# Seventy bf16 products with constants, whose results nobody reads, put on TensorE at six waits of a transformer kernel

## What is computed

```
x = x + attention(layernorm(x))        # 32 heads of 16, ALiBi bias, causal softmax, projection
x = x + moe(layernorm(x))              # 3 experts (tanh, gelu, silu), 2 of them chosen per batch
x = x + mlp(layernorm(x))              # silu(x Wg) with the half nearest to zero cut per row, times x Wu, times Wd
x = x + moe(layernorm(x))              # the same weights as before

# moe, per batch b: the two experts are those of the first token of the batch
router_input = concatenate([h, text_strength / vision_strength])
scores = softmax(router_input @ gate_w + gate_b)
out = sum_i top_val[i] * (act_e(h @ w1[e] + b1[e]) @ w2[e] + b2[e]),  e = top_idx[first token, i]
```

## Time and profile before

| | |
|---|---|
| time, 3 runs | 722.05, 723.75, 724.3 us; median 723.75 |
| the profiled execution | 721.25 us, of which the span of instructions is 719.5 us |
| TensorE busy | 664.0 us, 92% of the span |
| VectorE, ScalarE, GpSimd busy | 484.1, 338.8, 81.1 us |
| mean granted clock of TensorE | 0.984 of full speed |
| longest waits of TensorE after the first transpose | 3.8 us (L2005), 3.6 (L1627), 3.4 (L1802), 2.3 each (L2024, L1724) |

### The profile page before, as it was taken

The page is one execution under the profiler, slowest core; times in us unless marked ns, Lnnn a source line. Parts: engine busy times, 40 slices in busy tenths (PEclk is TensorE's granted clock), DMA queues, the critical chain, the costliest instruction groups (busy, mean ns, idle before and its releaser), DMA issues.

```text
span 719.5 us, 9856 instructions
## 1 busy us (share of the span) xinstructions
PE 664.0 (92%) x3656; PEld 480.4 (67%) x3656; DVE 484.1 (67%) x905; ACT 338.8 (47%) x520; POOL 81.1 (11%) x185
## 2 busy tenths in 40 slices
PE   4887999999988879999999899999999879999996
PEld 3665677677666557887777565665756555778775
DVE  6647595796589769786794636456365785868555
ACT  4203643612633663532459968466374804435231
POOL 4302002101200020001060010010100300100000
PEclk9989999999999999999999999999999989999999
DMA  8393511521844140000260000000004004000000
GB/s 295 102 267 115 166 46 47 155 67 38 257 148 152 72 158 1 0 1 1 92 221 3 0 1 0 1 2 0 0 1 160 16 0 176 2 29 15 15 30 30
DMA packets 31618, 51.85 MB, mean 72 GB/s; under 512 B 3289, under 2 KB 16988, under 8 KB 30015
## 3 DMA queue, kind: packets, MB, share of 16 engines
q1 hardware_dynamic: 31186, 49.64, 21.5%
q10 hardware_dynamic: 384, 1.57, 1.0%
HBM read 42.61 MB, written 8.40 MB: 71 GB/s over the span
## 4 chain that ended last, share of the span: by engine, by line
PE 77%; DVE 14%; DMA 2%; ACT 2%; issue 2%; SPq 1%; POOL 1%; ACTq 1%; DVEq 0%; POOLq 0%
PE ps L1835 13%; PE ps L1974 12%; PE ps L1802 12%; PE ps L2035 10%; PE ps L1627 7%; PE ps L1978 5%; DVE nmax L1060 3%; PE ps L1677 2%; PE ps L1743 2%; PE ps L1811 2%; DVE nmax L1057 1%; PE ps L1733 1%; DVE prodT L1561 1%; PE ps L1700 1%; PE ps L1804 1%
## 5 line engine op out<-in xcount | busy, mean ns | idle before, releaser
L2035 PE MATMUL ps<-wdT,prodT 128*128 128x512 f32 (+1 forms) x176 | 78.5, 602 | 0.4
L2035 PEld LDWEIGHTS ps<-wdT,prodT 128*128 128x128 f32 (+1 forms) x176 | 33.1, 192 | 41.2 <-issue 38.8
L783 ACT ACTIVATE probsT<-ps 128x1536 f32<-128x1536 f32 x32 | 46.1, 1449 | 23.6 <-PE ps L1733 23.4
L822 ACT ACTIVATE funs<-ps 128x512 f32<-128x512 f32 x16 | 9.6, 598 | 97.5 <-PE ps L1804 81.3
L1561 DVE COPY prodT<-ps 128x512 f32<-128x512 f32 (+1 forms) x24 | 13.8, 599 | 42.7 <-PE ps L2024 42.3
L1137 DVE SCALAR_TENSOR_TENSOR junk<-x_sb,gate_row 128x512 f32<-128x512 f32 x48 | 41.1, 857 | 1.0
L659 POOL TENSOR_SCALAR ln_spread<-ln_moments 128x1 f32<-128x1 f32 x24 | 7.7, 321 | 301.5 <-DVE ln_moments L1131 301.4
L1404 DVE SCALAR_TENSOR_TENSOR x_sb<-b_row,coef,x_sb 128x512 f32<-128x512 f32 x48 | 37.9, 790 | 1.7
L1060 DVE TENSOR_REDUCE nmax<-ps 128x4 f32<-128x1024 f32 x32 | 38.8, 1212 | 0.0
L756 ACT CAST parts<-ps 128x512 bf16<-128x512 f32 x16 | 9.1, 587 | 61.9 <-PE ps L1662 61.8
L949 ACT ACTIVATE sign_junk<-mlp_size_next,minus_guess 128x1376 bf16<-128x1376 f32 x24 | 34.6, 1443 | 0.8
(11 more groups left out here) (278 smaller groups left out, 1689.8 us busy)
## 6 DMA issues: line engine op xcount, KB each, us to landing
cuts<-parts SPq DMA_DIRECT2D x16, 384.0 KB, 3.1
qst<-cuts SPq DMA_DIRECT2D x48, 128.0 KB, 2.9
w_first_raw<-in_L_ffn_w SPq DMA_DIRECT2D x6, 1024.0 KB, 9.2
w_second_raw<-in_L_ffn_w SPq DMA_DIRECT2D x6, 1024.0 KB, 9.0
kst<-cuts SPq DMA_DIRECT2D x36, 128.0 KB, 2.7
wqkv_raw<-in_L_attn_a_w_attn SPq DMA_DIRECT2D x3, 1024.0 KB, 9.5
wdT<-in_L_attn_b_w_down SPq DMA_DIRECT2D x1, 2560.0 KB, 10.1
wg_raw<-in_L_attn_b_w_gate SPq DMA_DIRECT2D x1, 2048.0 KB, 8.3
```

The source lines that it names most:

```text
L783: nc.scalar.activation(probsT[:, g % 2, :].rearrange("p (k n) -> p k n", k=3), slot[g % 2], ACT.Exp).then_inc(exp_ok.sem, 1)
L2035: last = nc.tensor.matmul(ps[:, Y_BANK, :], prodT[0:m, c, :], wdT[0:m, c, :], start=(c == 0), stop=(c == IC - 1))
```

## The change

`fill(bank, n)` issues n products of `ident16` with `ones16`, the latter repeated four times to 512 columns, into one PSUM bank, each with `start=True` so that the bank is overwritten. No semaphore is counted up by them. It is called at six places, 70 products in all: 15 in front of the first query product of batch 1, 10 in front of the transposed scores of batch 0, 13 in front of the low product of row tile 1 in the first expert block, 16 in front of `check(7)`, 9 in front of `down(0)` and 7 in front of `down(6)`. Where the bank could still be read, the wait for its readers is put ahead (it stood behind that place before, in the instruction that follows).

```diff
+            def fill(bank, n):
+
+                for _ in range(n):
+                    nc.tensor.matmul(ps[:, bank, :].rearrange("p (h k) -> p h k", h=G), ident16[:, :],
+                                     diagonal(ones16, G), start=True, stop=True, skip_group_check=True)
@@ ffn_front
                     for k, (signal, a, part) in enumerate(products):
+                        if n == 1 and k == 2 and s == 0 and use == 0:
+                            fill(3, 13)
                         need(pe, signal, n, 1)
@@ attend
             def attend(b):
+                if b == 0:
+                    need(pe, nmT_ok, 0, 1)
+                    need(pe, res1, 1, 2)
+                    fill(0, 10)
                 need(pe, nm_in, b, nm_in.per)
@@ the order of attention
             turn_rows(1)
+            fill(0, 15)
             query(1, 0)
@@ check
             def check(n):
+                if n == T - 1:
+                    fill(4, 16)
                 need(pe, mlp.pick, n, 7)
@@ the loop of the gated block
                 if n == 0:
+                    need(pe, mlp.hT, 3, 2)
+                    fill(PROD_BANK[0], 9)
                     pe.wait_ge(wd_here, 32)
+                elif n == T - 2:
+                    need(pe, mlp.hT, T - 1, 2)
+                    fill(PROD_BANK[0], 7)
                 down(n)
```

## The result

The changed kernel takes 719.63 us (median of 16 runs, 717.46 to 722.72) against 723.75 (16 runs, 719.78 to 729.28). The ratio is 0.9948, with a 95% interval of 0.9924 to 0.9972: faster by 0.52%, some 3.8 us. The forecast was 717.3, a gain of 6.45; the direction was right, and the gain was a good half of it. The profiled execution took 719.5 us (before 721.25), only 1.75 us less where the sum said 5.5.

A forecast was written before the change was run, and what follows sets the result against it. TensorE was taken to bound the kernel, with its clock the whole question. Gains of 1.3 + 0.9 + 1.0 + 2.4 - 0.1 = 5.5 us gave 715.7 profiled; the median forecast was 717.3 us, range 714.0 to 721.6.

The forecast's parts named there:

- the sum: Gains at four places less 0.1 us for late fills: 5.5 us, taking the profiled execution from 721.25 to 715.7 us.
- the four falls: TensorE's clock at 0.50 from 37.10, 269.20, 405.74 and 586.64 us, within or right behind waits of TensorE.
- the fills don't keep the clock up: Rival, chance 0.10: identity products don't hold the clock, which falls as before; 722.7 us, or 725.2 by the median.
- the slower one: Rival, chance 0.05: fills run at the low clock, 0.44 us a product, 14 us late in all; 737 us.
- query product and `scores(0, 0)`: Batch 1's query product: TensorE free 2.7 us earlier, but scores wait for the gathered transfer; gain 1.3 us.
- expert block, row tile 1: TensorE 1.85 us ahead at full clock, then held by VectorE making `aT_lo`; gain 0.9 us, ends 0 and 1.85.
- `down(0)`: Its 22 instructions and the transposes with their copies at full clock: gain 1.0 us, TensorE going on without waiting.
- `up(7)`: 12 products in 2.79 us in place of 5.22: gain 2.4 us, VectorE's mask not late.
- fills in `attend(0)`: They end 0.4 us after the transfer released TensorE; the exponential has some slack, so a cost of 0.1 us.
- the forecast wait on `aT_lo`: Sign of being right: in the expert block's `ffn_back`, TensorE waits on `aT_lo` near 276 us.
- a part works: Rival, chance 0.15: clock still falls at one large place, or a transfer or VectorE takes back more; 719.7 us without `up(7)`.
- From the profiled execution to the median: Median 718.2 us if the 2.5 us difference is an offset, 715.7 if fills win back further falls; 717.3 taken.

The follow-up runs named there:

- group A: The change's 15 fills ahead of `query(1, 0)`, the first query product of batch 1.
- B: The change's 10 fills in `attend(0)`, ahead of the transposed scores of batch 0.
- C: The change's 13 fills in the first expert block, ahead of the low product of row tile 1.
- D: The change's 16 fills ahead of `check(7)`; a kernel with only these took 720.74 us, ratio 0.9976 to the kernel before.
- E: The change's 9 fills ahead of `down(0)`.
- F: The change's 7 fills ahead of row tile 6, at `down(6)`.
- the double group: The changed kernel with 32 in place of 16 fills ahead of `check(7)`: 722.75 us, ratio 1.0004 to the kernel before.
- the third set: Kernels timed on the same chip as the kernel before (722.71 us), among them the change a third time: 720.99 us, ratio 0.9970.
- the change without B: The changed kernel without the 10 fills in `attend(0)`, the 15 at the query product kept: 718.33 us, ratio 0.9938 to the kernel before.

## Why the prediction came out as it did

**That the clock is the question, and that the fills hold it: right.** No stretch of the changed kernel's profiled execution is at the low level before the last product; in the eight profiles with group A, and in all with B, C, D, E or F, the clock is full at the filled place. The moved waits without fills leave the four falls as they were. The rival "the fills don't keep the clock up" (0.10) is excluded, and so is the slower one: no group was seen to run at the low clock.

**What a fill costs: right.** 0.22 us was forecast, 0.23 measured. At the double group the part beyond the wait cost its time, 3.1 us late and 0.49% in the ratio.

**The sum, term by term** (from the table of differences):

| term | forecast | measured in the profiled executions |
|---|---|---|
| query product and `scores(0, 0)` | 1.3 | 0.1 to 0.2 |
| expert block, row tile 1 | 0.9 | 2.24 - 1.37 = 0.87 |
| `down(0)` | 1.0 | 1.52 - 0.46 = 1.06 |
| `up(7)` | 2.4 | 0.49 + 1.78 = 2.27 |
| fills in `attend(0)` | -0.1 | -0.06 |
| transposed scores of batch 1 | none | -0.84 |

Three terms are within 0.15 us, the forecast wait on `aT_lo` among them (0.53 us). TensorE begins the last group of `up(7)` 1.78 us early and has lost nothing of it at the last product. The sum of the right-hand side is 3.4, the measured gain 3.8; that they come so near is in part luck, since the one is of a single pair of executions and the other holds the falls that move as well.

**The step that failed** is "ScalarE's six issues run from 32.98 for 4.13 us; the last is begun at 32.98 + 5 x 0.69 = 36.4 and lands 6.0 us later, at 42.4", from which the 1.3 us followed. I took the last landing from one of the two queues. The gather is issued half on ScalarE and half on SyncE; SyncE's last issue was begun some 0.4 us later, took 6.7 us, and landed about 43.5. That the transfer is what is late next was right; its end was off by 1.1 us, and with it this term, from 1.3 to 0.1 or 0.2. From the first transpose of batch 1 to the scores it is 9.5 to 10.0 us in the eight profiles with A (mean 9.8) and 9.8 to 10.3 in the six without (mean 10.0), so the term is some 0.3 us in the mean.

The measured 719.63 us is also the price of the rival "a part works" (719.7, 0.15). Its number was worked out from a fall that stays at `up(7)`, which did not come; its other condition, a transfer that takes back more, did, at this term and at the next.

**What was not in the sum: the row maxima of batch 1.** Their transfer took 3.4 us for one of its three pieces where it had taken 2.2, and TensorE waited 0.73 us for it. That is -0.84 us in the profiled execution. The cause, as far as shown, is in the last section. In the third set the change without B was 0.32%, 2.3 us, ahead of the change (the intervals just meet), more than this one wait.

**From the profiled execution to the median: right in direction, wrong in size.** I let the kernel before lose more falls in its median run (723.75) than in the profiled one (721.25), and the change win all of them back. Part of them stand where no group is: at 18, 45, 250 and 537 us. Profiles of the change showed falls at 18, 45 and 250. So the changed kernel's median is not that of an execution without a fall either. The profiled executions of before and after also differ by 1.5 us that belong to no part of the change (0.5 ahead of the first fill, 1.0 at the gather at 200 us); in the twelve other profiles this second one was between -0.5 and +0.4. I cannot explain it, and it is why the two profiled executions are only 1.75 us apart while the medians are 4.1 apart.

The Trainium skill, "TensorE: Matmul & The Clock Gate", section "HAM oscillation — how this bites in real kernels", counts a stretch at the low clock as lost at half its length. For the four stretches of the earlier trace rows, 20.5 us, an estimate by that rule is 10.2 us of kernel time. By the table the four places gave back 4.3 to 4.4, so here the rule is a bound and not the price: TensorE had products in 17.25 us of the 20.5, and at the first place a transfer was late next.

## What to carry to other kernels

A wait of TensorE that lets its clock fall can be filled with small products that nobody reads, if they end before what is waited for; the gain is what the products behind were slowed by, less what the next-late thing takes back. Before you count a gain behind a wait, list every queue that delivers into the same semaphore and take the latest landing, not that of the queue you looked at first. If that landing is late anyway, filling ahead of it leaves a wait behind the fills, and the clock can fall there. Where falls move from run to run, collect their places from several executions before you choose where to fill: here two of the six groups were together worth nothing, and the lowest time came with three small groups in their stead, ahead of falls that the first profile did not show.

## What the runs showed of the hardware

**Instruction loads travel by DMA, and a small transfer beside one is late.** The view by queues has queues of their own for them; the 16 KB pieces of TensorE's stream are on q8. In the kernel before, such a piece began at 123.96 us, 4.3 us behind the last issue of the row maxima (119.7). In the changed kernel it began at 121.40, 1.35 us behind it (120.05), since the 25 fills put 50 instructions ahead. It lasts about 1 us. The changed kernel from 121.20 to 121.60 us and from 122.20 to 122.40, then the change without B from 123.25 to 123.90 (queue, kind: packets, MB, share of 16 engines):

```profile
q1 hardware_dynamic: 45, 0.02, 15.9%
q8 instruction: 1, 0.02, 13.7%
...
q1 hardware_dynamic: 3, 0.00, 5.2%
```

```profile
q1 hardware_dynamic: 48, 0.02, 10.4%
```

The last piece of the row maxima is 48 packets. In the changed kernel 45 of them begin as usual, none from 121.60 to 122.20, and the last 3 from 122.26 on, as the instruction packet (0.88 us long) ends. It is so in all seven profiles with 25 or more fills in the attention, where the long landing was 3.4 to 3.7 us in place of 2.1 or 2.2. In the seven with 15 or none all 48 have begun before the instruction piece does. That a few packets of the transfer stand behind the instruction packet is shown so, and the last run moved all 25 fills to one place and kept it. What decides it is not: the piece began 1.3 to 1.7 us behind the issue in the seven with the long landing, but also 1.6 behind it in the change without B, which had none (4.2 to 5.9 in the other six).

The Trainium skill, "Runtime: NRT & Kernel Launch", section "Instruction fetch mechanics", states that the stream is refilled in blocks of 16 KiB (256 instructions) and that the cost is mostly hidden. The size agrees with the 0.02 MB of one packet; that it is hidden did not hold for the transfer beside it.

**The places of the falls move.** Over these profiles they were at 18, 36 to 39, 45, 68, 250 to 254, 268 to 271, 405 to 408, 536 to 537, 575 and 587 to 592 us. The one at 18 comes behind a wait of 2 us for VectorE's split of the weights, the one at 45 behind the 2 us for the gather, the one at 250 to 254 behind three short waits (0.9, 1.2 and 0.7 us), the one at 536 to 537 some 2 us behind one of 0.7. The same waits stand in other executions without a fall. The mean granted clock and the time of an execution go together: for the kernel before, 0.986 with 720 to 722.5 us and 0.974 with 727 to 729; for the changed one, 0.999 or more with 717.5 to 719.6 and 0.991 with 722.4 to 722.8. So most of the spread between runs of one kernel goes with its clock, and, as far as the profiles show, with the number of its falls.
